# A fused AdaLN block with Infini-attention and a mixture of experts: the weight splitting is moved out of the routing stage

## The reference

```python
mod = (silu(c) @ wmod)                 # six rows per batch: shift, scale, gate for each half
h = layernorm(x) * (1 + ca) + sa
x = x + ga * infini_attention(h)       # 16 heads of 16, segments of 64 tokens, memory M, z per head
h = layernorm(x) * (1 + cb) + sb
x = x + gb * moe(h)                    # 8 experts, top 2 by softmax of the router
# attention, per segment:
A_mem = sigma(q) @ M / (sigma(q) . z + 1e-6);  A_dot = softmax(causal(q k^T / 4)) @ v
out   = beta * A_mem + (1 - beta) * A_dot
M    += sigma(k)^T (v - sigma(k) @ M / (sigma(k) . z + 1e-6));  z += sum sigma(k)
# expert:
gate, up = split(h @ w13[e]);  y = (silu(gate) * up) @ w2[e]     # w13: 256 x 1024, w2: 512 x 256
```

## Time and profile before

| what | value |
|---|---|
| median of 3 runs | 1364.13 us (1361.73 to 1368.67) |
| the profiled execution | 1369.12 us, of it a span of 1367.3 us |
| busy: TensorE, its weight loads | 87%, 74% of the span |
| busy: VectorE, ScalarE, GpSimd | 69%, 52%, 67% |
| mean granted TensorE clock | 0.929 of 2.4 GHz |
| attention | to about 671 us, with the set-up |
| routing | about 671 to 747 us |
| experts | about 748 us to the end |

### The profile page before, as it was taken

One profiled execution on the slowest core, in us unless ns is written; L12 is line 12 of the kernel. 1 busy time (PEld: TensorE's weight loads), 2 busy tenths in 40 slices (PEclk: granted clock), 3 DMA queues, 4 the chain that ended last, 5 costly groups with the idle time before them and its releaser, 6 DMA issues. The chain is left out here.

```text
span 1367.3 us, 54714 instructions
## 1 busy us (share of the span) xinstructions
PE 1189.4 (87%) x20150; PEld 1015.1 (74%) x20150; DVE 941.2 (69%) x2509; ACT 708.3 (52%) x1389; POOL 919.6 (67%) x997
## 2 busy tenths in 40 slices
PE   3489999999999999997322899999999999999995
PEld 0277777777877878776122799999999999999994
DVE  2389999898999999986498355555555555555552
ACT  2267888888888888885522222323322232222321
POOL 3048999998999999998310466666666666666643
PEclk8599999999999999998555899999999999999998
DMA  9911333333333333334653454545455455555540
GB/s 220 179 50 50 81 94 92 83 93 89 96 87 92 96 96 87 95 91 99 196 147 102 108 95 91 98 92 97 91 102 99 93 95 96 98 94 97 99 75 1
DMA packets 116414, 134.54 MB, mean 98 GB/s; under 512 B 17899, under 2 KB 95795, under 8 KB 116035
## 3 DMA queue, kind: packets, MB, share of 16 engines
q0 software_dynamic: 32848, 57.03, 22.5%
q1 hardware_dynamic: 83314, 74.02, 21.8%
HBM read 63.60 MB, written 44.04 MB: 79 GB/s over the span
## 5 line engine op out<-in xcount | busy, mean ns | idle before, releaser
L1333 PE MATMUL psum<-xT,w13s 128*128 128x256 f16 x3408 | 398.6, 274 | 3.5 <-DVE xT L1321 2.8
L1333 PEld LDWEIGHTS psum<-xT,w13s 128*128 x3408 | 332.1, 98 | 42.8 <-issue 4.3
L1400 POOL DMA_INDIRECT out<-yo,sidx x142 | 226.8, 1597 | 200.6 <-DVE yo L1390 172.1
L1342 ACT ACTIVATE sg<-psum 128x512 f32<-128x512 f32 x142 | 84.8, 597 | 317.3 <-PE psum L1333 301.7
L1348 DVE SCALAR_TENSOR_TENSOR hf<-psum,sg 128x512 f32<-128x512 f32 x142 | 98.2, 692 | 215.1 <-ACT sg L1342 205.5
L1302 POOL DMA_INDIRECT grow<-moe_rows,gidx x142 | 140.3, 988 | 97.2 <-SPq L1403 54.3
L1371 PE MATMUL psum<-w2s,hT 128*128 x1704 | 197.6, 273 | 0.3 <-DVE hT L1362 0.3
L1371 PEld LDWEIGHTS psum<-w2s,hT 128*128 128x128 f16 x1704 | 166.6, 98 | 19.9 <-issue 0.5
L1357 ACT ACTIVATE hT<-hf 128x512 f16<-128x512 f32 x142 | 89.4, 629 | 107.7 <-DVE hf L1348 104.7
L689 POOL TENSOR_TENSOR pT<-sc,pT 128x1024 f16<-128x1024 f32 x64 | 136.6, 2134 | 10.4 <-ACT pT L684 10.4
L1362 DVE TENSOR_TENSOR hT<-hf,hT 128x512 f16<-128x512 f32 x142 | 98.3, 692 | 56.8 <-ACT hT L1357 43.1
(11 more groups left out here) (215 smaller groups left out, 2405.9 us busy)
## 6 DMA issues: line engine op xcount, KB each, us to landing
stk<-qk SPq DMA_DIRECT2D x384, 64.0 KB, 2.7
moe_rows<-hrows SPq DMA_DIRECT2D x128, 128.0 KB, 2.4
stage<-in_w SPq DMA_DIRECT2D x24, 512.0 KB, 4.7
out<-xall SPq DMA_DIRECT2D x128, 64.0 KB, 2.1
xall<-in_x SPq DMA_DIRECT2D x8, 896.0 KB, 19.5
grow<-moe_rows,gidx POOLq DMA_INDIRECT x142
out<-yo,sidx POOLq DMA_INDIRECT x142
wmod_sb<-in_wmod SPq DMA_DIRECT2D x1, 1536.0 KB
```

The costliest lines, as they stand in the source:

```text
L1333: i = k.e.matmul(bank[:, n * LONG:(n + 1) * LONG], w13s[:, b_, bass.ds(ex_reg * (G * 2 * I) + (c * 2 * I + col), P)], xT[:, k.b, a, c, :], ...
L1342: done(k.e.activation(sg[:, half, :], bGate[half][:, :], ACT.Silu, scale=1.0 / W_SCALE), "sg")
L1400: k.e.indirect_dma_start(out_rows, bass.IndirectOffsetOnAxis(ap=sidx[:, n:n + 1], axis=0), yo[:, k.v, q, :], None, bounds_check=B * T - 1, ...
```

## The change

1. `xall` is allocated for the whole kernel, and the split `w13s` is laid over it: chunk i's high part and rest take the places of x tiles 4i to 4i+3, that is of segment i. TensorE's addresses of w13 change accordingly.
2. Chunks 0 to 13 of w13 are loaded and split inside the attention, one chunk per round: the load (512 KB) at the end of SyncE's rounds 58 to 71, the high part at the end of ScalarE's rounds 63 to 76, the rest at the end of VectorE's rounds 66 to 79. Load i waits until segment i of all four pairs is stored, and, as there are three landing buffers (`NRAW`), from load 3 on until the rest of chunk i-3 is made.
3. `store` waits for the earlier output store of the same pair, and the output stores have a semaphore per pair.
4. In the routing stage chunks 14 and 15 are split where two rests were before; w2's high parts are made there by ScalarE, and its rests (eight instructions) move to VectorE's first two steps of the experts. `down` of slot 0 waits for them. No rest is left between the groups.
5. `RING` grows from 16 to 32 (four groups), and the tile numbers and the 1 that they are multiplied with are float16.

```diff
+NCH, NEARLY, NRAW = E * G, 14, 3
+ROUND_LOAD, ROUND_HI, ROUND_LO = NT - 6, NT - 1, NT + 2
-RING, NHOT = 16, 8
+RING, NHOT = 32, 8
+def w13_part(w13s, i, a):
+    return w13s[:, (2 * i + a) * 2 * I:(2 * i + a + 1) * 2 * I]
+def w13_high(e, w13s, raw, i):
+    return e.activation(w13_part(w13s, i, 0), raw, ACT.Copy, scale=W_SCALE)
+def w13_low(e, w13s, raw, i):
+    return e.scalar_tensor_tensor(out=w13_part(w13s, i, 1), in0=raw, scalar=W_SCALE, in1=w13_part(w13s, i, 0),
+                                  op0=ALU.mult, op1=ALU.subtract)
...
     def store(k):
...
+        if k.s > 0:
+            k.e.wait_ge(s_out[k.j], k.s * 32)
...
+    def raw_load(e, i):
+        for j in range(4):
+            e.wait_ge(s_out[j], 32 * (i + 1))
+        if i >= NRAW:
+            e.wait_ge(s_rlo, i - NRAW + 1)
+        e.dma_start(raw[:, i % NRAW, :], w13_chunk(w13, i)).then_inc(s_raw[i % NRAW], 16)
+    def raw_high(e, i):
+        e.wait_ge(s_raw[i % NRAW], 16 * (i // NRAW + 1))
+        w13_high(e, w13s, raw[:, i % NRAW, :], i).then_inc(s_rhi, 1)
+    def raw_low(e, i):
+        e.wait_ge(s_rhi, i + 1)
+        w13_low(e, w13s, raw[:, i % NRAW, :], i).then_inc(s_rlo, 1)
+    chunk_work = {"sync": (ROUND_LOAD, raw_load), "scalar": (ROUND_HI, raw_high), "vector": (ROUND_LO, raw_low)}
     def engine_program(name, e):
...
             for lag, stage in stages:
                 if 0 <= i - lag < NT:
                     stage(Tile(e, i - lag, full))
+            if work and 0 <= i - first < NEARLY:
+                work(e, i - first)
...
-            for i in range(EARLY):
-                weight_rest(i)
+            for i in range(NLATE):
+                e.wait_ge(s_hi, i + 1)
+                w13_low(e, w13s, late13[:, i, :], NEARLY + i)
...
-                for i in range(left * k // groups, left * (k + 1) // groups):
-                    weight_rest(EARLY + i)
...
     def down(k):
...
+        if k.t == 0:
+            k.e.wait_ge(s_w2lo, E)
...
+            w2_low(range(4))
             for t in range(-1, NSLOTS + 1):
                 now, ahead, late = slot(e, t), slot(e, t + 1), slot(e, t - 1)
+                if t == 0:
+                    w2_low(range(4, E))
```

More of the change, by code:

```diff
@@ L354, in attention @@
     h2 = sb("h2", [P, 2, D])
+    raw = sb("raw", [P, NRAW, 2 * I])
     h2T = sb("h2T", [P, 2, 2, G, P], F16)
@@ L374, in attention @@
     s_stk = [sem(f"s_stk{j}") for j in range(4)]
-    s_out = sem("s_out")
+    s_out = [sem(f"s_out{j}") for j in range(4)]
+    s_raw, s_rhi, s_rlo = [sem(f"s_raw{i}") for i in range(NRAW)], sem("s_rhi"), sem("s_rlo")
     s_st = [sem(f"s_st{j}") for j in range(4)]
@@ L955, in engine_program @@
         deepest = max(lag for lag, _ in stages)
-        for i in range(NT + deepest):
+        first, work = chunk_work.get(name, (0, None))
+        rounds = max(NT + deepest, first + NEARLY) if work else NT + deepest
+        for i in range(rounds):
             full = deepest < i < NT
@@ L967, in _ @@
                 e.wait_ge(s_st[j], 32 * NS)
-            e.wait_ge(s_out, 32 * NT)
+            for j in range(4):
+                e.wait_ge(s_out[j], 32 * NS)
         @block.tensor
@@ L987, in experts @@
 def experts(nc, ctx, sb_, sem_, banks, trib, iota, number, count, tok_id, out_rows, rows_dram,
-            w13, w2, idh, logits, passed):
+            w13, w13s, w2, idh, logits, passed):
     def sb(name, shape, dt=F32):
@@ L1037, in experts @@
     s_tab, s_tabTr, s_tabT = sem("r_tab"), sem("r_tabTr"), sem("r_tabT")
-    s_wl, s_hi, s_lo = [sem(f"r_wl{i}") for i in range(NSTAGE)], sem("r_hi"), sem("r_lo")
-    chunks = [(w13[e_, c * P:(c + 1) * P, :], w13s, (e_ * G + c) * 1024) for e_ in range(E) for c in range(G)]
-    chunks += [(w2[e_].rearrange("(k p) n -> p k n", p=P), w2s, e_ * KC * D) for e_ in range(E)]
+    s_13, s_2 = [sem(f"r_13_{i}") for i in range(NLATE)], [sem(f"r_2_{i}") for i in range(E)]
+    s_hi = sem("r_hi")
     bBefore, bTotal, bTab, bTr, bFound = banks[0], banks[1], banks[2:4], banks[4], banks[5]
@@ L1050, in _ @@
         def _(e):
[L1051 to L1057, removed]
+            for i in range(NLATE):
+                e.dma_start(late13[:, i, :], w13_chunk(w13, NEARLY + i)).then_inc(s_13[i], 16)
+            for i in range(E):
+                e.dma_start(raw2[:, i, :].rearrange("p (k n) -> p k n", k=KC),
+                            w2[i].rearrange("(k p) n -> p k n", p=P)).then_inc(s_2[i], 16)
         @block.vector
@@ L1068, in by_token @@
                 return ap.rearrange("p e t -> p t e")
[L1070 to L1076, removed]
             lg, rank = logits[:, :, :], bc(iota[:, 2, 0:E], NT)
             e.memset(one[:, :], 1.0)
+            e.memset(one16[:, :], 1.0)
             e.memset(seen[:, 0:1], 0.0)
@@ L1181, in _ @@
         def _(e):
[L1182 to L1190 removed]
+            for i in range(NLATE):
+                e.wait_ge(s_13[i], 16)
+                w13_high(e, w13s, late13[:, i, :], NEARLY + i).then_inc(s_hi, 1)
+            e.wait_ge(s_gap, 2)
+            e.activation(ex[:, :, :], gap[:, :, :], ACT.Exp).then_inc(s_exp, 1)
+            e.activation(e2[:, :], e2[:, :], ACT.Exp).then_inc(s_exp, 1)
+            for i in range(E):
+                e.wait_ge(s_2[i], 16)
+                e.activation(w2s[:, 0, i * 1024:(i + 1) * 1024], raw2[:, i, :], ACT.Copy, scale=W_SCALE).then_inc(s_w2hi, 1)
             for half in range(2):
@@ L1216, in _ @@
                     for i in range(NGRP):
-                        mm = e.matmul(bCol[:, i:i + 1], numbers[:, i * P:(i + 1) * P], one[0:1, :], start=True, stop=True)
+                        mm = e.matmul(bCol[:, i:i + 1], numbers[:, i * P:(i + 1) * P], one16[:, :], start=True, stop=True)
                     mm.then_inc(s_tcol, 1)
```

38 lines of the change are left out of this document (21 added, 17 removed).

## The result

The changed kernel takes 1384.44 us (median of four runs, 1374.73 to 1389.01) beside 1366.04 for the kernel before: a ratio of 1.0128 with an interval of 1.0067 to 1.019. It is slower, by some 12 to 18 us; the forecast was 7. Its profiled execution took 1383.87 us, with a span of 1382.0 us for 1367.3 and a mean granted clock of 0.923 for 0.929.

What follows compares the result with a forecast made beforehand. Four engines were nearly full in the attention, VectorE alone bound routing, and TensorE was never idle in the experts' stage. +22.3 + 7.8 - 23.0 = +7.1 us on 1364.1 gave 1371 us; range for 8 of 10, 1353 to 1388.

Steps and rivals of the forecast that it cites:

- The place and the kind of the loss: Attention's last rounds: from load 3 SyncE waits for rests ahead of `stack_low`, delaying `row_max` of tile 63 by +22.3 us.
- the ring: Attention's last rounds: VectorE's and SyncE's rounds become one chain without overlap, once per round, from load 3 on.
- The length of a held round: Attention's last rounds: load issue 0.8, stacks to `row_max` 6.8, to round's end 3.7, rest 1.3; 12.6 us per round.
- The start: Attention's round 66: rest 0 ends at 583.55 us, and loads 0 to 2 add 1.5 us, giving 585.05.
- The emptying pipeline: Attention's end, behind `row_max` of tile 63: last high parts, rests, load 13 and stores add +7.8 us (4 to 10).
- The routing stage: Routing: 20 rests off VectorE save 22.4 us and less waiting for tile numbers 0.6; saving 23.0 (22 to 24).
- The experts' first steps: Experts' first two steps: the moved w2 rests fit into VectorE's idle time; cost nothing, at most 1 us.
- Rival 1, the lock: Attention's last rounds: VectorE's rests and GpSimd block each other reading SBUF; +3 and +5, 1379 us, chance 0.18.
- Rival 2, stacks not late: Attention's last rounds: SyncE's hold is shorter, a round's chain under about 10.5 us; +11, 1352 us, chance 0.19.
- Rival 3, the clock: Attention's last rounds: gaps lower TensorE's granted clock, 14.5 us a round, +10 on the sum; 1382 us, chance 0.10.
- Rival 4: Routing stage: TensorE or ScalarE holds the groups, only 16 of 23 us go; 1378 us, chance 0.08.
- the likeliest case: Whole kernel: the forecast itself, +7.1 us to 1371 us, own range 1362 to 1380, chance 0.45.

Runs made afterwards that it cites:

- e1: Changed kernel with high parts and rests of chunks 0 to 13 one round earlier; 1353.47 us, 0.9937 of the kernel before.
- e2: Changed kernel with the loads one round later on SyncE; 1352.02 us, 0.9927 of the kernel before.
- e4: Changed kernel with loads 0 to 13 cut to 64 of 1024 columns (32 KB), waits kept; 1358.07 us in one run, beside 1356.93 for the kernel before.
- e10: Changed kernel with tile numbers written in order, loads two rounds later and behind `stack_low` in SyncE's round; 1343.25 us, 0.9834 of the kernel before.
- e3: Kernel before plus only a one-column memset ending VectorE's rounds 66 to 76 and SyncE's wait for it; 1370.43 us, 1.0059 of the kernel before.
- e9: Changed kernel run again without edit, five rounds; 1377.16 us, 1.0085 of the kernel before.
- e8: e2 with the float16 tile numbers written in order, in runs of eight neighbours; 1353.66 us, 0.9921 of the kernel before.

## Why the prediction was right, and where its sizes were off

- **The place and the kind of the loss: right.** The first load that waits (number 3) begins the ring at round 66, and `row_max` follows the stack issues. e1 and e2 are the proof: with one round of slack SyncE's wait for a rest is gone from these rounds, and 22 to 24 of the 32.8 us with it.
- **The length of a held round: mis-sized, 12.6 for 14.16 us.** This is the term of the sum that failed. Counted as the forecast did, from a rest's end to the next one's, it is (657.64 - 586.85) / 5. Its parts, in the mean of these five rounds: rest's end to first stack issue 0.5 us (taken 0.8); from there to `row_max` 8.2 (7.8 to 8.6; taken 6.8); `row_max` to the round's end 4.05 (taken 3.7); the rest 1.4 (taken 1.3 with its wake-up). I had averaged three rounds of before in which nothing large stood ahead of the stacks in the queue; e4 shows that the load's transfer is worth 2 us there. Five rounds make 7.8 us. The last part, from the end of round 71 (656.20 + 1.44 = 657.64) to `row_max` of tile 63, is 7.6, just the forecast's 0.8 + 6.8: no `stack_high` follows there, and from its first stack issue to `row_max` it is 7.0 us. The start is 1.8 (rest 0 ended at 586.85, the forecast had 585.05). With the 0.9 by which the body was earlier this is the 10.5 us between +22.3 and +32.8.
- **The emptying pipeline: right**, +7.7 for +7.8. The attention ends with a store of `out` (707.05 us), as said, and no longer with the logits. It comes out by the steps that were forecast: from `row_max` of tile 63 to the issue of load 13 30.0 us (forecast 30.3), to the end of the last store's issue 43.1 (forecast 42.8).
- **The routing stage: right**, -21.9 for -23.0. The 1.1 us and more are the strided float16 writes (3.5 us for 1.6 before), which I had priced at nothing; that SyncE and ScalarE had more to do there held up nobody.
- **The experts' first steps: hidden, as said.** The stretch is even 1.8 us shorter.
- **Rival 1, the lock:** there, at little more than 1 us for the 8 that it was given. **Rival 2, stacks not late:** false for this kernel, and much of what e1, e2 and e10 make true; the limit that I gave it, a ring of under about 10.5 us, is met by the bare ring of e3 (10.06), and even that one costs 8 us. Its sum was wrong as well: 8 less 3 us in the rounds, 1.5 for the first loads and 7.8 at the end are +14, not +11, by its own terms, and the time 1355, not 1352. **Rival 3, the clock:** in part, and more than the forecast allowed. The granted clock is 0.86 from 600 to 640 us, and 0.50 to 0.72 from `row_max` to the round's end; against the 3.15 us at full clock in e4 that is 0.8 to 1.0 us a round, of which the forecast's 3.7 had about half. A held round took 14.2 us in the mean and 14.7 at most, near rival 3's 14.5, but more of the excess over 12.6 is the load's transfer. **Rival 4:** false.

All in all the forecast of +7 was right in its sign; +18.4 and (e9) +12.4 us were measured, and 1384.44 and 1377.16 both lie in the range that was given, but 1384.44 lies above the likeliest case's own 1362 to 1380, nearest to rival 3's 1382; the error of one term, 10 us, is larger than the forecast effect, because two large terms cancel. The term itself, +32.8, lies at the upper edge of its bounds (+14.7 to +33.5), and that e9's time is close to those of rivals 1 and 4 (1379, 1378) is chance, as neither is what happened. What stays open: why profiled executions are up to 13.6 us apart before tile 54, why e8's ScalarE is late, and which of e10's two changes gave how much.

## What to carry to other kernels

In a pipeline written out by hand, a wait in the queue that issues the DMAs is a wait of everybody whose data stands behind it: count the rounds between the event that it waits for and the first use of what is queued behind it, and leave at least one round. Put a large prefetch behind the small transfers that somebody is waiting for, not ahead of them, even when the DMA engines have time to spare over a whole round: for these few us they haven't. And where the engines are all less busy after work was added, look for a ring before you blame the added work.

## What the runs showed of the hardware

- A 512 KB load issued right ahead of four to six DMAs of 64 KB on one queue: these land in 4.3 us in the median for 2.7 with a load of 32 KB, and their user starts 2 us later (8.0 for 6.0 us). The DMA busy share is 0.87 in the five us behind the load, 0.47 over the rounds.
- A VectorE instruction with two inputs in SBUF and a GpSimd instruction of 0.55 us with two, begun within it: the latter takes 1.53 us; the former 1.44 in the median for 1.21. Beside a VectorE memset of 0.48 us the GpSimd instruction keeps its 0.55.
- From `row_max` to a held round's end TensorE's work takes 3.98 us at a granted clock of 0.68 and 4.17 at 0.50, and 3.15 at 1.00 in e4.
- 512 float16 results in one partition: 2280 ns spread out (32 bytes from one to the next), 1001 ns in runs of eight; for the instruction behind it, 1224 and 281 ns. In float32, spread out (64 bytes), 1003 and 583. Spread out, the narrower type was the slower one.
- `row_max` of tile 54 started between 539.0 and 552.6 us in twelve profiled executions, at 551.6 and 551.3 us in the two of the changed kernel. Whether that belongs to the kernels or to the single executions no run shows; whole executions of one kernel differ as much (1357.22 to 1373.39 us in 14 of the kernel before). A stretch between equal instructions leaves that part out of a comparison of two profiles.
